# Token rows that carry their own gates, and a second fetch that adds on chip, in a graph layer with a mixture of experts

## What is computed

```python
x = x + _L0_gnn_ref(_layernorm(x), src, dst, W, b)      # gather rows by edge, sum by target, matmul, relu
...
probs = softmax(xt @ Wr + br)
top_p, top_idx = top_k(probs, 2)
weights = top_p / top_p.sum(-1)
h = gelu(einsum(xe, W1) + b1)                            # 256 -> 1024, for each expert
y = einsum(h, W2) + b2                                   # 1024 -> 256
out = (weights[:, :, None] * sel).sum(axis=1)            # the two experts of each token
x = x + out
```

## Time and profile before

| | us |
|---|---|
| three runs, median | 1667.14 |
| lowest and highest | 1662.34, 1669.77 |
| the profiled execution | 1664.14 |
| its span | 1662.7 |
| granted TensorE clock, mean | 0.821 |

### The profile page before, as it was taken

One profiled execution on the slowest core, in us unless ns is written; L12 is line 12 of the kernel. 1 busy time (PEld: TensorE's weight loads), 2 busy tenths in 40 slices (PEclk: granted clock), 3 DMA queues, 4 the chain that ended last, 5 costly groups with the idle time before them and its releaser, 6 DMA issues.

```text
span 1662.7 us, 26613 instructions
## 1 busy us (share of the span) xinstructions
PE 1195.6 (72%) x9098; PEld 987.7 (59%) x9098; DVE 951.2 (57%) x2502; ACT 594.8 (36%) x1169; POOL 1123.3 (68%) x1116
## 2 busy tenths in 40 slices
PE   6954565647358545995499649969849768689995
PEld 5954344535146224982498439858728746578894
DVE  8997456656434353656265735764745648455552
ACT  4954011111032003440344025515315335455662
POOL 5006777777777777777777777777777757864233
PEclk9999565657578557996799779979959968899998
DMA  6027866775475447974787469769569579999982
GB/s 187 1 101 266 263 220 209 223 241 171 125 265 161 108 118 262 310 222 131 260 275 251 137 224 313 254 203 303 172 199 300 163 240 243 281 308 269 278 250 61
DMA packets 196730, 356.06 MB, mean 214 GB/s; under 512 B 25476, under 2 KB 94630, under 8 KB 196596
## 3 DMA queue, kind: packets, MB, share of 16 engines
q1 hardware_dynamic: 130008, 205.39, 36.7%
q0 software_dynamic: 60224, 142.57, 30.0%
q10 hardware_dynamic: 6364, 6.40, 1.2%
HBM read 290.80 MB, written 65.38 MB: 214 GB/s over the span
## 4 chain that ended last, share of the span: by engine, by line
PE 34%; DMA 26%; POOL 19%; issue 10%; DVE 7%; ACT 3%; SPq 0%; POOLq 0%; DVEq 0%; ACTq 0%
DMA gt<-zt,srcI 13%; PE ps L1260 9%; POOL gt L830 8%; PE ps L1159 8%; PE ps L1245 8%; DMA out<-gt,toks 5%; POOL xs L858 5%; DMA out<-acc 3%; POOL out L890 2%; PE ps L1134 2%; PE ps L1170 2%; DVE ohl L1334 2%; PE ps L1197 2%; POOL S L877 2%; DMA xb<-xs 1%
## 5 line engine op out<-in xcount | busy, mean ns | idle before, releaser
L830 POOL DMA_INDIRECT gt<-zt,srcI x832 | 834.2, 1003 | 254.1 <-issue 176.7
L1159 PE MATMUL ps<-gt,S 128*128 128x257 f16 x1664 | 349.3, 332 | 204.3 <-DMA gt<-zt,srcI 202.7
L1159 PEld LDWEIGHTS ps<-gt,S 128*128 128x128 f16 x1664 | 202.8, 151 | 306.4 <-DMA gt<-zt,srcI 291.2
L1245 PE MATMUL ps<-xe,w1b 128*128 128x256 f16 x2688 | 343.4, 282 | 34.5 <-DVE xe L1650 16.8
L1260 PE MATMUL ps<-w2b,hT 128*128 128x256 f16 x2688 | 316.7, 275 | 15.9 <-DVE yb L1682 8.2
L1245 PEld LDWEIGHTS ps<-xe,w1b 128*128 128x128 f16 x2688 | 270.0, 101 | 77.5 <-issue 20.0
L1106 ACT ACTIVATE h<-ps,cb 128x256 f32<-128x256 f32 x448 | 227.1, 557 | 245.9 <-PE ps L1245 244.8
L1656 DVE SCALAR_TENSOR_TENSOR hT<-h,cb,hT 128x512 f16<-128x512 f32 x224 | 167.7, 750 | 234.8 <-ACT hT L1110 234.2
L1260 PEld LDWEIGHTS ps<-w2b,hT 128*128 128x128 f16 x2688 | 264.7, 99 | 50.8 <-issue 15.7
L1110 ACT ACTIVATE hT<-h,cb 128x512 f16<-128x512 f32 x224 | 161.7, 722 | 7.3
L1084 ACT ACTIVATE aT<-ps 128x256 f32<-128x256 f32 x98 | 37.4, 381 | 319.5 <-PE ps L1190 319.5
(11 more groups left out here) (261 smaller groups left out, 1249.6 us busy)
## 6 DMA issues: line engine op xcount, KB each, us to landing
w1b<-ws SPq DMA_DIRECT2D x56, 1024.0 KB, 6.5
w2b<-ws SPq DMA_DIRECT2D x56, 1024.0 KB, 8.7
ws<-w2b SPq DMA_DIRECT2D x16, 1024.0 KB, 4.9
xb<-xs SPq DMA_DIRECT2D x56, 260.0 KB
gt<-zt,srcI POOLq DMA_INDIRECT x832, 4.0
ys<-yb SPq DMA_DIRECT2D x34, 256.0 KB, 7.0
w1b<-in_L_ffn_W SPq DMA_DIRECT2D x8, 1024.0 KB, 8.5
hT<-in_L_ffn_W SPq DMA_DIRECT2D x8, 1024.0 KB, 12.9
```

Source lines behind the costliest of these rows:

```text
L830: e.indirect_dma_start(out=gt[:, i % NG, :], out_offset=None, in_=zt, in_offset=bass.IndirectOffsetOnAxis(ap=srcI[:, c, r:r + 1].bitcast(u ...
L1159: inst = e.matmul(PS[r % 2][:, 0:257], S[:, r % NS, :, c], gt[:, i % NG, part * 257:part * 257 + 257], start=(c == 0 and part == 0), stop= ...
L1245: inst = e.matmul(UP[n % 2][:, z * BS:(z + 1) * BS], w[:, l, kk, j * 128:(j + 1) * 128], xe[m % 2][:, k, kk, :], start=(kk == 0 and l == 0 ...
```

## The change

The gates are now multiplied into the rows of all blocks, also of those that are stored: `y` of blocks 0 to 33 gets the three small gate instructions and the two multiplications (now L1654 to L1676), and `st` waits for them. VectorE's step `cc` is gone, with the spare buffers and the copies of the gates. A tile's first fetch is a plain gather that writes its rows `row(t)` of `acc`; the second is a gather with `compute_op=add` into the same rows, which must wait for the first. The two fetches go in batches: the first fetches of tiles 0 to 9, those of the next batch ahead of or among the second fetches of this one, with one semaphore for each of the four batches. A buffer `xb` is loaded anew when its block's `y` is done, for all blocks, and no longer after the transposes. The planner has new costs for Pool (1.3 for a first fetch, 1.9 for a second, 3.7 for a `give`, 2.0 for a `sums`), lets a fetch or a scatter into `xs` be listed only when Pool's clock is at most 0.3 ahead, and keeps fetches out of the last microsecond before the serial chain is expected to be free.

```diff
 def fetch_stages():
-    yield [[("cg", t, (("POOL", 2.5),)), ("cc", t, (("DVE", 1.1),))] for t in range(TG)]
+    turn = [(0, 0)]
+    for b in range(NSUM):
+        turn += [(b + 1, 0)] * (b + 1 < NSUM) + [(b, 1)]
+    for b, i in turn:
+        yield [[("cg", (t, i), (("POOL", 1.9 if i else 1.3),))] for t in range(*SUMS[b])]
...
-                after(end, "y", m, (("DVE", 0.85 if m < M0 else 1.7),), lambda e: over(m, e))
+                after(end, "y", m, (("DVE", 1.7),), lambda e: over(m, e))
...
-        if max(s["chain"], s["base"]) > s["now"] or clock["POOL"] > s["now"] + 2.6:
+        if max(s["chain"], s["base"]) > s["now"] or clock["POOL"] > s["now"] + 0.5:
             return False
         if batches and batches[0][0] <= s["now"]:
             b = batches.popleft()[1]
-            emit("sums", b, (("POOL", 1.3 * (SUMS[b][1] - SUMS[b][0])),), s["now"])
+            emit("sums", b, (("POOL", 2.0),), s["now"])
+            s["chain"] = clock["POOL"] + 3.0 + 1.1 * (SUMS[b][1] - SUMS[b][0])
             s["summed"] += 1
         elif gives and (BLOCKS[gives[0]][0] < LAST or s["late"] <= s["now"]):
-            emit("give", gives.popleft(), (("POOL", 3.4),), s["now"])
+            emit("give", gives.popleft(), (("POOL", 3.7),), s["now"])
+            s["chain"] = clock["POOL"] + 4.5
             s["given"] += 1
         else:
             return False
-        s["chain"] = clock["POOL"] + 5.0
         return True
...
-                if kind == "cg" and clock["POOL"] > s["now"] + 2.5:
+                if kind in ("cg", "xs") and (clock["POOL"] > s["now"] + 0.3 or (gives or batches) and s["now"] + 1.0 < max(s["chain"], s["base"]) + 1.0 < s["now"] + 2.0):
...
-                if kind == "cc" and any(arg == b1 - 1 for b0, b1 in SUMS):
-                    batches.append((end, [b1 - 1 for b0, b1 in SUMS].index(arg)))
+                if kind == "cg" and arg[1] and any(arg[0] == b1 - 1 for b0, b1 in SUMS):
+                    batches.append((end + 5.0, [b1 - 1 for b0, b1 in SUMS].index(arg[0])))
...
-                chain.at = end + 2.0 if kind == "cg" else s["now"] if kind == "xs" else end
+                chain.at = s["now"] if kind == "xs" else end
...
-            fetches.append(Job(fetch_stages(), s["now"], width=NC - 1))
+            fetches.append(Job(fetch_stages(), s["now"]))
...
                 elif kind == "cg":
-                    t = arg
-                    if t == 0:
+                    t, i = arg
+                    b = next(b for b, (b0, b1) in enumerate(SUMS) if b0 <= t < b1)
+                    if t == i == 0:
                         e.wait_ge(s_pick, 1)
                         e.wait_ge(s_zero, 16)
-                        e.wait_ge(s_tile, R * CT)
+                        e.wait_ge(s_base, 16 * BASE_DMAS)
                         for z in range(NY):
                             e.wait_ge(s_yst[z], 16 * ((M0 - z + NY - 1) // NY))
-                    if t == NCS + NCT:
-                        for z in range(NSC):
-                            e.wait_ge(s_sc[z], sent(LAST - 1, z))
-                    if t >= NC:
-                        e.wait_ge(s_comb, t - NC + 1)
-                    for i in range(2):
+                    if i == 0:
                         e.indirect_dma_start(
-                            out=fetched_rows(t, i), out_offset=None, in_=ys,
-                            in_offset=bass.IndirectOffsetOnAxis(ap=cidx[:, i, t:t + 1].bitcast(u32), axis=0)
-                        ).then_inc(s_cg[t % NC], 16)
+                            out=row(t), out_offset=None, in_=ys,
+                            in_offset=bass.IndirectOffsetOnAxis(ap=cidx[:, 0, t:t + 1].bitcast(u32), axis=0)).then_inc(s_cg[b], 16)
+                    else:
+                        if t == SUMS[b][0]:
+                            e.wait_ge(s_cg[b], 16 * (SUMS[b][1] - SUMS[b][0]))
+                        e.indirect_dma_start(
+                            out=row(t), out_offset=None, in_=ys,
+                            in_offset=bass.IndirectOffsetOnAxis(ap=cidx[:, 1, t:t + 1].bitcast(u32), axis=0),
+                            compute_op=ALU.add).then_inc(s_cg[b], 16)
                 elif kind == "give":
                     m = arg
                     a = m - M0
-                    e.wait_ge(s_y, a + 1)
+                    e.wait_ge(s_y, m + 1)
...
-                    e.wait_ge(s_comb, b1)
+                    e.wait_ge(s_cg[arg], 32 * (b1 - b0))
...
-                    e.wait_ge(s_yread, m + 1)
+                    e.wait_ge(s_y, m + 1)
...
-                    if NX <= m < M0 + NX:
-                        e.wait_ge(s_xT, m - NX + 1)
-                    elif m >= M0 + NX:
-                        e.wait_ge(s_y, m - NX - M0 + 1)
+                    if m >= NX:
+                        e.wait_ge(s_y, m - NX + 1)
...
-                    e.tensor_copy(wts[:, 0, cs], xrow[:, bs, 257])
-                    e.tensor_copy(wts[:, 1, cs], xrow[:, bs, 258])
...
+                    x4, mine = xb[m % NX], cb[m % 3][:, 11:12]
                     if a >= 0:
-                        x4, mine = xb[m % NX], cb[m % 3][:, 11:12]
                         e.tensor_copy(toks[:, a, :], x4[:, :, 256].bitcast(i32))
-                        e.scalar_tensor_tensor(out=gate[:, 0, :], in0=x4[:, :, 259], scalar=mine, in1=x4[:, :, 257],
-                                               op0=ALU.is_equal, op1=ALU.mult)
-                        then(e.scalar_tensor_tensor(out=gate[:, 1, :], in0=x4[:, :, 259], scalar=mine, in1=x4[:, :, 258],
-                                                    op0=ALU.not_equal, op1=ALU.mult))
-                        e.tensor_tensor(gate[:, 2, :], gate[:, 0, :], gate[:, 1, :], ALU.add)
+                    e.scalar_tensor_tensor(out=gate[:, 0, :], in0=x4[:, :, 259], scalar=mine, in1=x4[:, :, 257],
+                                           op0=ALU.is_equal, op1=ALU.mult)
+                    then(e.scalar_tensor_tensor(out=gate[:, 1, :], in0=x4[:, :, 259], scalar=mine, in1=x4[:, :, 258],
+                                                op0=ALU.not_equal, op1=ALU.mult))
+                    e.tensor_tensor(gate[:, 2, :], gate[:, 0, :], gate[:, 1, :], ALU.add)
...
-                    if m >= M0:
-                        e.wait_ge(s_yread, m + 1)
-                        for z in range(2):
-                            inst = e.tensor_scalar(o[:, z, :], o[:, z, :], gate[:, 2, z:z + 1], None, ALU.mult)
-                        inst.then_inc(s_y, 1)
-                elif kind == "cc":
-                    t = arg
-                    e.wait_ge(s_cg[t % NC], 32 * (t // NC + 1))
-                    if t == 0:
-                        e.wait_ge(s_base, 16 * BASE_DMAS)
-                    then(e.tensor_scalar(row(t), fetched_rows(t, 0), wts[:, 0, t:t + 1], None, ALU.mult))
-                    e.scalar_tensor_tensor(out=row(t), in0=fetched_rows(t, 1), scalar=wts[:, 1, t:t + 1], in1=row(t),
-                                           op0=ALU.mult, op1=ALU.add).then_inc(s_comb, 1)
+                    e.wait_ge(s_yread, m + 1)
+                    for z in range(2):
+                        inst = e.tensor_scalar(o[:, z, :], o[:, z, :], gate[:, 2, z:z + 1], None, ALU.mult)
+                    inst.then_inc(s_y, 1)
```

14 lines of the change are left out of this document (1 added, 13 removed).

## The result

Over 22 runs each, the kernel before takes 1664.25 us (median; 1658.88 to 1670.69) and the changed one 1672.17 us (1666.12 to 1681.03). The ratio is 1.0042, with a 95% interval of 1.0031 to 1.0053. The change makes the kernel 0.4% slower; the prediction had it 0.6% faster. The profiled execution of the changed kernel took 1681.03 us, the slowest of its 22, with a span of 1679.5 us.

The account below looks back on a forecast made before the run. Pool bounds the kernel up to the last gather, then TensorE and Pool's serial chain, the chain binding at the end. Chain end 1650 + 3 gives a span of 1653, 0.994 of before; forecast 1656 us, 8-in-10 range 1638 to 1676.

Parts of the forecast that it names:

- Step 1: Up to the last gather at 1337: VectorE's added gate work lengthens Pool's gathers, +3 us, with 0 and 21 as ends.
- The port rival: Up to the last gather: VectorE's multiplications fully block Pool through a port; 1656 + 18 = 1674 us, chance 0.05.
- Step 2: Start of the fetches, waiting for the last stored block to land: +2 us, between -4 and +7.
- Step 3: Pool's list up to the last chunk: second fetches cost 25 us more, yet block 38 is transposed some 6 us earlier.
- Step 4: VectorE without cc, 1420 to 1545: TensorE's 16.7 us of waits go, its last block ends about 22 us earlier.
- Step 5: Serial chain: start stays at 1383.9, fourth sums start at 1570.4, last give at 1640, span ends at 1650.
- Step 6: DMA engines, 1377 to 1556: second fetches add 19 us of all engines, taken as covered, bound +20.
- The second rival: Accumulating fetches load full DMA engines from 1400 to 1560, up to 20 us on the chain; 1676 us, chance 0.13.
- The fourth rival: Nothing gained: the chain keeps its 26 steps and its idle grows with Pool's second fetches; 1665 us, chance 0.12.
- The packed chain: First rival: the chain's 15 idle us vanish and TensorE's 1641 binds; 1640 to 1648 us, chance 0.18.

Follow-up runs that it names:

- the stores first: Changed kernel with the stores of blocks 32 and 33 ahead of block 34's loads on SyncE: 1926.99 us, 1.0013; with larger planner chain costs too: 1931.13 us, 1.0042.
- the second group: Follow-up runs on a chip where the kernel before takes 1922.2 us; the changed kernel, unaltered, measured 1928.57 us there, ratio 1.0018.
- the holds: Changed kernel with up weights of some blocks held until a sums landed: second and third sums 1907.36 us, 1.0027; fourth as well 1911.36 us, 1.0047.
- half weights: Only half of each block's weights loaded from block 38 on: kernel before 1653.39 us, 0.9931; changed kernel 1649.34 us, 0.9893, and 1907.45 us, 0.9924, on another chip.
- two holds: Changed kernel with the up weights of blocks 44 and 48 held until the second and third sums had landed: 1907.36 us, 1.0027.
- TensorE slower: Changed kernel with the first twelve up multiplications of blocks 38 to 48 done twice: 1675.32 us, 1.0047.

## Why the prediction was wrong

**What bounds the kernel** was read rightly: two lines of work that end close together, with the chain as the one that binds. The failure is in how long the chain's steps take once the other line is relieved.

**Step 1** is right, and its closeness is partly luck. The last gather goes out at 1340.06, 3.1 us later than before, where +3 was taken, but in four profiles on the 1922 us chips with the same work up to there it lies between 1565.5 and 1573.3. The port rival falls. Gathers take 1006 ns on average instead of 1003. Where the multiplications cover 4 columns the mean is 993 ns, against 1002 in the changed kernel and 1000 with the stores first on the same chip. The last gather is at 1566.6 there and at 1566.9 with the stores first, and the whole gets 2 us shorter, within the uncertainty. The rule of the Trainium skill (SBUF — State Buffer, Who interferes with whom), by which a multiplication of this kind can block Pool fully, does not show here as the 21 us that it could have made.

**Step 2** was too small, and at a place where the forecast gave it no weight. The first fetch came 7.1 us later, at the bound of +7. The store was ready at 1334 but stood on SyncE behind the loads of block 34, and was issued at 1341.70. It cost the chain no more than the 4.2 us by which its first give came later, where the forecast left it in place. Whether these 4.2 us reach the end stays open, since the runs with the stores first were made where the first give waits for block 34 anyway.

**Step 3** is right in the price: second fetches stand 1.87 us apart, the upper of the two bounds. The last piece of chunk 7's scatter did not come 54 us after the first fetch but 55.4 (1411.38), and with the later first fetch that is 3.9 us later than before, where the forecast had it 2.6 earlier (4.6, less the 2 of step 2). Block 38 was transposed at 1417.5, 3 us earlier than before and not 6.

**Step 4** is right in the mechanism and not in the size. TensorE's large waits for VectorE are gone. Its last result came 9 us earlier and not 22. Of the difference of 13, 3 us are those of step 3, and TensorE's waits for block inputs and second weights, 4.0 and 1.5 us before from 1400 to 1640, are now 9.0 and 4.8, 8 us more. Some 2 us are left unexplained:

```profile
PE ps L1229 <- DMA xb<-xs: 4.0, 1, 4.0
PE ps L1260 <- DMA w2b<-ws: 1.5, 2, 1.3
```

(These are the rows of before; those of after stand in the section on the result.)

**Step 5** is the term that failed: it carried the durations of the chain's steps over from the trace of the kernel before. It expected the last give at 1640 (1639.7 by its own terms) and it came at 1670.1. These 30.4 us are: 4.2 for the start; 8.7 for the 13 gives up to the fourth sums (147.2 us, where 123.5 and 15 of idle were taken); 11.3 for the first three sums (59.3 instead of 48); 4.3 for the fourth (22.0 instead of 17.7); and 2.0 for the gives behind it. In this execution half of the error is one number: the sums, taken at 16 and 17.7 us from a trace in which TensorE ran slower and asked for fewer weights beside them. In the second group's profile of the same kernel the sums take 11 us less and the gives 7 more. What holds in both is the whole chain, 282.0 and 277.6 us from first to last give, where step 5 had 256 and the kernel before took 268.7. The second part is in the gives, since the second and third started 15.0 and 17.0 us behind the one before. They waited for nothing but Pool's own list: the second stood behind three second fetches and four pieces of the scatter, which kept Pool busy to 1402.8, though the give before had landed at 1396:

```profile
1396.03 1.54 POOL L870 DMA_INDIRECT acc<-ys,cidx  x1 [0.30 <-DMA out<-yb,toks]
...
1401.84 0.98 POOL L849 DMA_INDIRECT xs<-xrow,slI  x1 [0.30 <-issue]
1403.13 1.59 POOL L883 DMA_INDIRECT out<-yb,toks  x1 [0.30 <-issue]
```

**Step 6** said "covered", and that is not so, though the second fetches are not its main part. Bytes that weighed on the chain were the weights', on the sums beside them (the holds) and on the gives too (half weights). The addition in the second fetch costs 2 to 7 us of the 20 that were its bound. The second rival came nearest to what happened: load on the DMA engines stretches the chain, with sums of 19 us instead of 16, and a time of 1676, at a chance of 0.13. The three later sums were above 19 in the profiled execution, but the median is 1672, and the rival blamed the accumulating fetches and not the weights. Its other threshold, gives of 10.6 us, says nothing: up to the fourth sums they took 11.3 us on average, waits included, and by the same measure 11.4 in the kernel before.

The fourth rival, that nothing is gained, put the time at 1665, 7 us below the median and without the traffic as a cause. The packed chain did not come about.

## What to carry to other kernels

When a stall is taken off an engine that fetches its operands anew for every block, ask when those bytes will move now, and what serial chain they will then run beside. A step's duration read from the old trace holds only for the old traffic.

Where two lines of work end within a few microseconds of one another, relieving the one that does not set the end gave nothing here. The experiment is cheap: give that line back what it won (16 us of extra multiplications here) and see whether the time moves.

Before an experiment on another chip is taken for an answer, look in its trace whether the wait in question is there at all. The stores first were tried where Pool had 22 us to spare.

## What the runs showed of the hardware

- A large accumulating write into DRAM (1.3 MB, the fourth 1.4) took 15.1 to 18.1 us beside 0.08 to 0.14 MB a microsecond of weights and block inputs, in the kernel before, the changed one (both chips) and the one with two holds. Beside 0.15 to 0.20 it took 16.8 to 22.8. The rate alone does not settle it: with TensorE slower the fourth took 16.8 us beside 0.20 MB a microsecond, in the changed kernel 22.0 beside as much. With almost no weights beside it (0.42 and 0.55 MB in all, two holds) it took 16.2 and 15.1, with Pool's own queue at 90 and 95% of the engines; the third sums of the kernel before with half weights took 12.2 beside 0.62 MB.
- The same transfer without the addition took 14 to 16 us, and 12 for the last, at 0.18 to 0.23 MB a microsecond. It went in 368 packets for 1.44 MB, against 1424 with the addition.
- An indirect gather with an addition into SBUF holds Pool 1.55 + 0.30 us, against 0.95 + 0.30 for a plain one. An accumulating scatter into DRAM holds it as long (1.55 to 1.59 + 0.30).
- The same program took 1664, 1903 or 1922 us on different chips, and the difference lay mostly ahead of the last gather (1340.1 and 1573.3 in the changed kernel). The ratios of the changed kernel (1.0042 and 1.0018) and of its half-weight form (0.9893 and 0.9924) differ by 0.3% between the two kinds of chip. The waits did not stay the same: the first give waits 22 us for block 34 on the one and not at all on the other.
